# A relational graph kernel whose head is rearranged: which queue brings the constants, how early loads are sent, and in which slots seeds, message weight and looks stand

## The chip, the cores and the metric

The kernel runs on one core of one Trainium2 chip, in one launch. The metric is device time in microseconds (us). Before the change it is 169.39, the median of 3 runs (169.31 to 169.51). Engines are TensorE (PE), VectorE (DVE), ScalarE (ACT), GpSimd (POOL) and SyncE (SP). Five instruction streams run at once and meet only at semaphores.

## The reference

There are 128 graphs of 128 nodes with 128 features, and an adjacency matrix of integers for each. In this data its entries are 0 and 1. The reference computes two layers:

```
vals = (x @ W_loop.T + b_loop) * sigmoid((x @ W_loop.T) @ Wg_loop.T + bg_loop)
x1   = layernorm(x  + relu(adj_t(==1)  @ vals))          # other relations: entries 2..40
out  = layernorm(x1 + (adj(==1) @ x1) @ W_msg[0] + bias)   # other weights: entries 2..4
```

The layer norms are over features, without scale and shift. Entries above 1 are served by a general path (behind a flag) that this data doesn't take; the "looks" below are the check for it.

## The kernel before, in words

The 128 graphs are worked in 32 groups of 4, so a tile is 128 partitions x 512 float32 values (256 KB). Every engine walks the same loop of slots, t = 0 to 31. In slot t the stages stand for different groups, with lags written out by hand:

- `project(t)` (PE, L379): for each graph x_t times `w_gate` (128 x 256) into `hg_ps`, which has two halves used in turn. The left half of `w_gate` is `w_loop_t`; the right half is the product `w_loop` x `wg_t`, folded by PE at the start and copied by DVE (L641). The matmul accumulates onto biases that were written into `hg_ps` beforehand: the seed (ACT, L515, `seed`; for half of group 0 also DVE, L638), a copy of `gate_b`. A seed of group q may only be written when the `vals` of group q-2 have been taken from the same half.
- `gates(t)` (ACT, L524): sigmoid of the right part. `values(t)` (DVE, L727): the product `vals`.
- `loop_sum(t-1)` (PE, L391): adjacency times `vals`. `first_sum` (DVE, L735): relu and the addition of x, giving `s_sb`. `first_stats` (L742), the chain of small operations for the inverse root (L665 to L691, `chain`), and `norm1` (POOL, L320 and L328) give x1.
- `messages(t-3)` (PE, L409), `copy_messages` (ACT, L534), `message_weights(t-4)` (PE, L430), `second_sum` (DVE, L753), `second_stats` (L757), `norm2` (ACT, L551, in two halves `(0, 1)` and `(2, 3)`), and the store (SP, L258).
- `look(t)` (ACT, L560) squares the adjacency less one half and sums it, to find entries above 1.

PE's order in a slot is project, loop_sum, message_weights, messages. ACT's is copy_messages, half of norm2, gates(t), seed(t+1), the other half of norm2, look(t). In DVE's slots the whole inverse-root chain stands before `values` while there is no second sum (up to slot 4).

The weight of the second layer, `w1`, is centred by `message_weight` (DVE, L647 to L656, waiting on `w1_in`), one PE matmul with a constant matrix (L440, in slot 2) and `message_weight_end` (L661). DVE does the first in slot 1, between `values(1)` and `first_sum(0)`, and the last in slot 3.

Loads: SP sends `wg_t`, then x_t and x alternately into rings of 6 (L245, L250), one after another until the rings make it wait. ACT sends `w_loop`, `gate_b` (the biases) and `w_loop_t`, and after the first seed `w_msg`, `msg_bias` (`b1`) and `identity`. POOL waits for the two fold weights (`fold_in`, L334), then sends adjacency and transposed adjacency in pairs of groups (512 KB, L303, L310), the first five at once, and one more in each slot. PE begins with matmuls on a constant tile `warm`, 4 before `marked`, 3 more, and 3 after the fold.

Of the kernel before, what the change touches and what calls it, by code (L numbers as in the profile page):

```python
# [45 lines left out]
def exists(q):  # L46
    return 0 <= q < GROUPS
# [12 lines left out]
def build(nc, x, x_t, adj, adj_t, w_in, w_loop_t, wg_loop_t, gate_bias, w_msg, msg_bias,  # L60
          w_rel_t, wg_rel_t, b_rel, bg_rel, w_msgs, rel_ids, identity, out):
    with ExitStack() as ctx:
# [30 lines left out]
        w_gate = sb("w_gate", [P, 2 * P], F32)  # L93
        w_loop = sb("w_loop", [P, P], F32)
        wg_t = sb("wg_t", [P, P], F32)
        w1_raw = sb("w1_raw", [P, P], F32)
        w1 = sb("w1", [P, P], F32)
        b1 = sb("b1", [P, P], F32)
# [4 lines left out]
        warm = sb("warm", [P, W], BF16)  # L103
# [11 lines left out]
        ident = sb("ident", [P, P], F32)  # L115
# [27 lines left out]
        w_gate_in = sem("w_gate_in")  # L143
        fold_in = sem("fold_in")
        w1_in = sem("w1_in")
# [33 lines left out]
        ident_in = sem("ident_in")  # L179
# [61 lines left out]
        def _(sp):  # L241
# [21 lines left out]
            load_x(0)  # L263
            load_xt(2)
            load_x(1)
            load_xt(3)
# [30 lines left out]
        def _(pool):  # L297
# [35 lines left out]

            pool.wait_ge(fold_in, 16 * 2)  # L334
            load_adj(0)
            load_adj(1)
# [20 lines left out]
        def _(pe):  # L357
# [3 lines left out]
            for k in range(4):  # L361
                last = nc.tensor.matmul(bank[k], warm[:, 0:P], warm[:, :], start=True, stop=True)
# [4 lines left out]
            nc.tensor.matmul(aux_ps[:, 0:P], w_loop[:, :], wg_t[:, :], start=True, stop=True).then_inc(fold_done, 1)  # L367
# [6 lines left out]
            def project(q):  # L374
                if exists(q):
                    pe.wait_ge(xt_in[q % XT_RING], arrived(q, XT_RING))
                    pe.wait_ge(seeded, q + 1)
                    for b in range(GB):
                        last = nc.tensor.matmul(hg_ps[:, q % 2, b, :], xt_sb[:, q % XT_RING, batch(b)], w_gate[:, :],  # L379
                                                start=False, stop=True, skip_group_check=True)  # L380
                    last.then_inc(hg_done, 1)
# [31 lines left out]
            def message_weights(q):  # L413
                if exists(q):
                    if q == 0:
                        pe.wait_ge(w1_mid, 6)

                    if q in y_place:
                        pe.wait_ge(vals_done, GROUPS)
                    else:  # L420
                        await_count(pe, z_done, q)
                    if q >= LAST:
                        if q == LAST:
                            pe.wait_ge(ident_in, 16)
# [31 lines left out]
            def relation(step, ways):  # L456
                pe.wait_ge(rel_vals, step)
                for way in ways:
                    for b in range(GB):
                        last = nc.tensor.transpose(bank[way][:, batch(b)], gvals_t[:, way, batch(b)], ident[:, :])  # L460
# [39 lines left out]
        def _(act):  # L500
            act.dma_start(w_loop[:, :], w_in).then_inc(fold_in, 16)
            act.dma_start(gate_b[:, :], gate_bias).then_inc(bias_in, 16)
            act.dma_start(w_gate[:, 0:P], w_loop_t).then_inc(w_gate_in, 16)
# [51 lines left out]
            def look(q):  # L555
                spot = q // 2 % ADJ_RING
                act.wait_ge(adj_in[spot], arrived(q // 2, ADJ_RING))

                await_count(act, seen_done, q)
                nc.scalar.activation(seen[:, :], adj_sb[:, 2 * spot + q % 2, :], ACT.Square, bias=half[:, 0:1],  # L560
                                     accum_out=seen_sum[:, q:q + 1]).then_inc(seen_done, 1)

            seed(0)
            act.dma_start(w1_raw[:, :], w_msg).then_inc(w1_in, 16)
            act.dma_start(b1[:, :], msg_bias).then_inc(w1_in, 16)
            act.dma_start(ident[:, :], identity).then_inc(ident_in, 16)
            for t in range(GROUPS):
# [3 lines left out]
                seed(t + 1)  # L571
                norm2(t - NORM2_LAG, (2, 3))
                look(t)
# [53 lines left out]
        def _(dve):  # L627
# [13 lines left out]
            nc.vector.tensor_copy(w_gate[:, P:2 * P], aux_ps[:, 0:P]).then_inc(weights_ready, 1)  # L641

            def message_weight():


                dve.wait_ge(w1_in, 16 * 2)
                nc.vector.bn_stats(mid_stat[:, 0, :], w1_raw[:, :])  # L647
                nc.vector.bn_stats(mid_stat[:, 1, :], b1[:, :]).then_inc(w1_mid, 1)
# [156 lines left out]

            for t in range(GROUPS + 1):
# [82 lines left out]
            def general_pair(pair):  # L889
                dve.wait_ge(gadj_in, (pair + 1) * 32)  # L890
                for half_ in range(2):
# [25 lines left out]
                    for b in range(GB):  # L917
                        last = tt(gsum[:, batch(b)], gsum[:, batch(b)], b1[:, :], ALU.add)
# [56 lines left out]
```

## Time and profile before

| what | value |
|---|---|
| median of 3 runs | 169.39 us |
| profiled execution, its own time | 168.68 us |
| its span, first to last instruction | 166.9 us |
| busy share PE / DVE / ACT / POOL | 91% / 88% / 75% / 47% |
| mean granted TensorE clock | 0.985 of full speed |
| moved by DMA | 42.76 MB, mean 256 GB/s |
| share of the chain that ended last: PE / DMA / DVE | 78% / 8% / 7% |

The span is what the trace shows; the execution's time has 1.8 us around it. Shares of busy time are averages over a head, a long regular middle and a tail; which of them a change touches decides what it is worth. In the chain a piece is what the next one waited for. Start times are in us from the first instruction. A matmul of float32 data is recorded as two instructions, so four graphs give x8.

### The profile page before, as it was taken

The numbers are of one execution on the slowest core, as the hardware profiler recorded it, in microseconds if no ns is written. First come the engines' busy times: TensorE is split into PE (matmuls) and PEld (weight loads), VectorE is DVE, ScalarE is ACT, GpSimd is POOL, SyncE is SP. The second block draws the span as 40 slices with busy tenths as digits, with TensorE's granted clock in tenths as the row PEclk, the third lists the DMA queues.
The fourth block names the chain that finished last, engine by engine and source line by source line (L and its number), as shares of the span: only waits on it lengthen the run. The fifth ranks groups of instructions, "written<-read, shape, count | busy, mean of one in ns | idle before, by whom it ended". The sixth has DMA issues, their size and how long they took to land.

```text
span 166.9 us, 3913 instructions
## 1 busy us (share of the span) xinstructions
PE 151.6 (91%) x1072; PEld 140.4 (84%) x1072; DVE 146.7 (88%) x583; ACT 126.0 (75%) x287; POOL 78.6 (47%) x192
## 2 busy tenths in 40 slices
PE   6864899999999999999999999999999999998920
PEld 2553689999999999999999999999999999997910
DVE  1225999999999999999999999999999999999771
ACT  3266455679888888888888889998888888844661
POOL 2700366155555555565555555555554544446000
PEclk9999999999999999999999999999999999999985
DMA  4999999965999999999999899999995341131133
GB/s 137 342 389 394 397 401 403 308 196 189 298 302 306 310 304 274 280 312 301 268 305 329 272 277 333 325 310 298 253 324 212 85 166 63 65 130 63 64 125 138
DMA packets 19465, 42.76 MB, mean 256 GB/s; under 512 B 2160, under 2 KB 3056, under 8 KB 19440
## 3 DMA queue, kind: packets, MB, share of 16 engines
q1 hardware_dynamic: 13968, 25.24, 44.0%
q0 software_dynamic: 4608, 16.78, 33.2%
q10 hardware_dynamic: 864, 0.46, 0.9%
q8 instruction: 10, 0.16, 0.4%
q14 instruction: 15, 0.12, 0.3%
HBM read 34.08 MB, written 8.39 MB: 254 GB/s over the span
## 4 chain that ended last, share of the span: by engine, by line
PE 78%; DMA 8%; DVE 7%; issue 3%; ACT 1%; ACTq 0%; DVEq 0%
PE hg_ps L379 28%; PE msg_ps L409 16%; PE y_ps L430 15%; PE loop_ps L391 15%; DMA b<-msg_bias_dram 5%; DMA gate_b<-gate_bias_dram 2%; PE hg_ps L430 2%; PE hg_ps L426 2%; DVE s_sb L735 2%; DVE stats L742 1%; PE y_ps L426 1%; PE hg_ps L409 1%; ACT out_sb L551 1%; DVE z_sb L753 0%; DVE tiny L679 0%
## 5 line engine op out<-in xcount | busy, mean ns | idle before, releaser
L379 PE MATMUL hg_ps<-w_gate,xt_sb 128*128 128x256 f32 x256 | 60.8, 380 | 2.6 <-ACT hg_ps L515 2.5
L328 POOL TENSOR_SCALAR x<-s_sb,rstd,nmr 128x128 f32<-128x128 f32 x125 | 54.7, 446 | 3.7 <-DVE rstd L691 0.4
L379 PEld LDWEIGHTS hg_ps<-w_gate,xt_sb 128*128 128x128 f32 x256 | 46.2, 190 | 8.5 <-issue 3.0
L320 POOL TENSOR_TENSOR nmr<-mean_neg,rstd 128x4 f32<-128x4 f32 x31 | 6.0, 194 | 68.8 <-DVE rstd L691 68.8
L551 ACT ACTIVATE out_sb<-z_sb,rstd 128x128 f32<-128x128 f32 x112 | 38.0, 391 | 0.2 <-DVE rstd L691 0.2
L391 PEld LDWEIGHTS loop_ps<-vals,adj_sb 128*128 128x128 f32 x256 | 33.3, 191 | 5.2 <-issue 3.8
L391 PE MATMUL loop_ps<-vals,adj_sb 128*128 128x128 f32 x256 | 34.0, 276 | 2.6 <-DVE s_sb L735 2.6
L524 ACT ACTIVATE gate<-hg_ps 128x512 f32<-128x512 f32 x32 | 19.1, 597 | 22.2 <-PE hg_ps L379 22.1
L515 ACT ACTIVATE hg_ps<-gate_b 128x1024 f32<-128x1024 f32 (+1 forms) x32 | 32.3, 1010 | 1.0 <-DMA gate_b<-gate_bias_dram 1.0
L409 PE MATMUL msg_ps<-adjt_sb,x 128*128 128x128 f32 x248 | 33.0, 276 | 0.0
L430 PE MATMUL y_ps<-w,msg_t 128*128 128x128 f32 x232 | 30.6, 275 | 0.0
L409 PEld LDWEIGHTS msg_ps<-adjt_sb,x 128*128 128x128 f32 x248 | 30.2, 192 | 0.2 <-issue 0.2
L430 PEld LDWEIGHTS y_ps<-w,msg_t 128*128 128x128 f32 x232 | 28.2, 192 | 0.0
L727 DVE TENSOR_TENSOR vals<-hg_ps,gate 128x512 f32<-128x512 f32 x32 | 22.0, 688 | 6.4 <-ACT gate L524 5.7
L742 DVE BATCH_NORM_STATS2 stats<-s_sb 128x6 f32<-128x256 f32 x64 | 26.5, 426 | 0.3
L757 DVE BATCH_NORM_STATS2 stats<-z_sb 128x6 f32<-128x256 f32 x56 | 23.7, 427 | 0.0
L560 ACT ACTIVATE seen<-adj_sb,half 128x512 bf16<-128x512 f32 x32 | 22.7, 710 | 1.3 <-DMA adj_sb<-adj_dram 1.3
L534 ACT ACTIVATE msg_t<-msg_ps 128x512 f32<-128x512 f32 x31 | 18.0, 581 | 6.6 <-PE msg_ps L409 6.6
L735 DVE SCALAR_TENSOR_TENSOR s_sb<-loop_ps,x_sb 128x512 f32<-128x512 f32 x32 | 21.8, 682 | 0.0
L753 DVE TENSOR_TENSOR z_sb<-y_ps,x 128x512 f32<-128x512 f32 x28 | 19.1, 682 | 0.0
L303 POOL DMA_DIRECT2D adj_sb<-adj_dram x16 | 9.6, 598 | 2.8 <-DMA wg_t<-wg_loop_t_dram 2.8
L310 POOL DMA_DIRECT2D adjt_sb<-adj_t_dram x16 | 9.5, 591 | 0.0
(66 smaller groups left out, 104.9 us busy)
## 6 DMA issues: line engine op xcount, KB each, us to landing
xt_sb<-x_t_dram SPq DMA_DIRECT2D x32, 256.0 KB, 4.9
x_sb<-x_dram SPq DMA_DIRECT2D x32, 256.0 KB, 5.0
adj_sb<-adj_dram POOLq DMA_DIRECT2D x16, 512.0 KB, 5.5
adjt_sb<-adj_t_dram POOLq DMA_DIRECT2D x16, 512.0 KB, 5.2
out<-out_sb SPq DMA_DIRECT2D x32, 256.0 KB, 4.1
gate_b<-gate_bias_dram ACTq DMA_DIRECT2D x1, 128.0 KB, 3.4
w_loop<-w_loop_dram ACTq DMA_DIRECT2D x1, 64.0 KB, 2.0
wg_t<-wg_loop_t_dram SPq DMA_DIRECT2D x1, 64.0 KB, 2.2
```

Of the source, the lines that this page charges most:

```text
L328: last = nc.gpsimd.tensor_scalar(x1[:, q % X1_RING, batch(b)], s_sb[:, q % S_RING, batch(b)], r[:, b:b + 1], n[:, b:b + 1], ALU.mult, ALU.add)
L379: last = nc.tensor.matmul(hg_ps[:, q % 2, b, :], xt_sb[:, q % XT_RING, batch(b)], w_gate[:, :], start=False, stop=True, skip_group_check=True)
L391: last = nc.tensor.matmul(loop_ps[:, batch(b)], adj_sb[:, spot, batch(b)], vals[:, q % 2, batch(b)], start=True, stop=True)
L409: last = nc.tensor.matmul(msg_of(q)[:, batch(b)], x1[:, q % X1_RING, batch(b)], adjt_sb[:, spot, batch(b)], start=True, stop=True)
L430: last = nc.tensor.matmul(y_of(q)[:, batch(b)], msg_t[:, q % 2, batch(b)], w1[:, :], start=q < LAST, stop=True, skip_group_check=q >= LAST)
L515: nc.scalar.activation(hg_ps[:, q % 2, 0:graphs, :], gate_b[:, None, :].broadcast_to([P, graphs, 2 * P]), ACT.Copy).then_inc(seeded, 1)
L551: last = nc.scalar.activation(out_sb[:, q % OUT_RING, batch(b)], src, ACT.Copy, scale=r)
L560: nc.scalar.activation(seen[:, :], adj_sb[:, 2 * spot + q % 2, :], ACT.Square, bias=half[:, 0:1], accum_out=seen_sum[:, q:q + 1]).then_inc ...
L727: tt(vals[:, q % 2, :].rearrange("p (b n) -> p b n", b=GB), hg_ps[:, q % 2, :, 0:P], gate[:, q % 2, :].rearrange("p (b n) -> p b n", b=GB) ...
L735: stt(s_sb[:, q % S_RING, :], loop_ps[:, :], 0.0, x_sb[:, q % X_RING, :], ALU.max, ALU.add)\
L742: got = nc.vector.bn_stats(stats[:, (q + NORM1_LAG) % STATS_RING, p, :], s_sb[:, q % S_RING, 2 * p * P:2 * (p + 1) * P].rearrange("p (i n) ...
L757: got = nc.vector.bn_stats(stats[:, (q + STAT2_LAG) % STATS_RING, 2 + p, :], z_sb[:, q % Z_RING, 2 * p * P:2 * (p + 1) * P].rearrange("p ( ...
```

## The change

- Inputs are joined on the host: `w_loop` and `w_loop_t` to `w_loop_both` (one transfer of 128 KB into `w_all`, whose last third takes the folded product); `w_msg`, `msg_bias` and `identity` to `consts` (one transfer of 192 KB into `const_sb`).
- POOL no longer waits for the fold weights. It sends `gate_b`, `consts` and adjacency 0, waits for x_t 1, and then sends the other first loads. In the loop it sends both kinds of adjacency in odd slots, none in even ones.
- ACT sends only `w_loop_both`.
- SP waits for x_t 0 before it sends x_t 2, for x_t 1 before x 1, and for adjacency 0 before x_t 3 and all that follows.
- DVE does `message_weight` before slot 0 and `message_weight_end` at the end of slot 1. The matmul between them stands on PE in slot 1 before loop_sum(0).
- ACT seeds groups 0 and 1 before slot 0, and group t+2 at the end of slot t. `look(t - 1)` stands before that seed, and the last look after the loop.
- `warm` is a quarter as wide and is read repeatedly; of the matmuls on it 4 + 2 are left of 4 + 3 + 3.

```diff
 # SP
             load_xt(0)
             load_xt(1)
             load_x(0)
+
+            sp.wait_ge(xt_in[0], 16)
             load_xt(2)
+            sp.wait_ge(xt_in[1], 16)
             load_x(1)
+            sp.wait_ge(adj_in[0], 16)
             load_xt(3)
...
 # POOL
-            pool.wait_ge(fold_in, 16 * 2)
+            pool.dma_start(gate_b[:, :], gate_bias).then_inc(bias_in, 16)
+            pool.dma_start(const_sb[:, :], consts).then_inc(consts_in, 16)
             load_adj(0)
+            pool.wait_ge(xt_in[1], 16)
             load_adj(1)
...
-                if t % 2 == 0:
+                if t % 2 == 1:
                     load_adj(t // 2 + 3)
-                else:
                     load_adjt(t // 2 + 2)
...
 # PE
-            for _ in range(3):
-                nc.tensor.matmul(aux_ps[:, :], warm[:, 0:P], warm[:, :], start=True, stop=True)
             pe.wait_ge(fold_in, 16 * 2)
-            for _ in range(3):
-                nc.tensor.matmul(msg_ps[:, :], warm[:, 0:P], warm[:, :], start=True, stop=True)
-            pe.wait_ge(w_gate_in, 16)
+            for _ in range(2):
+                nc.tensor.matmul(msg_ps[:, :], warm[:, :], warm_wide, start=True, stop=True)
...
                 project(t)
+                if t == 1:
+                    pe.wait_ge(w1_mid, 3)
+                    nc.tensor.matmul(aux_ps[:, P:2 * P], share[:, :], w1_raw, start=True, stop=True)\
+                        .then_inc(w1_mean, 1)
                 loop_sum(t - LOOP_LAG)
-                if t == 2:
-                    pe.wait_ge(w1_mid, 3)
-                    nc.tensor.matmul(aux_ps[:, P:2 * P], share[:, :], w1_raw[:, :], start=True, stop=True)\
-                        .then_inc(w1_mean, 1)
...
 # ACT
-            act.dma_start(w_loop[:, :], w_in).then_inc(fold_in, 16)
-            act.dma_start(gate_b[:, :], gate_bias).then_inc(bias_in, 16)
-            act.dma_start(w_gate[:, 0:P], w_loop_t).then_inc(w_gate_in, 16)
+            act.dma_start(w_all[:, 0:2 * P], w_loop_both).then_inc(fold_in, 16)
...
             seed(0)
-            act.dma_start(w1_raw[:, :], w_msg).then_inc(w1_in, 16)
-            act.dma_start(b1[:, :], msg_bias).then_inc(w1_in, 16)
-            act.dma_start(ident[:, :], identity).then_inc(ident_in, 16)
+            seed(1)
             for t in range(GROUPS):
                 copy_messages(t - Y_LAG)
                 norm2(t - NORM2_LAG, (0, 1))
                 gates(t)
-                seed(t + 1)
                 norm2(t - NORM2_LAG, (2, 3))
-                look(t)
+                look(t - 1)
+                seed(t + 2)
+            look(GROUPS - 1)
...
 # DVE
+            message_weight()
             for t in range(GROUPS + 1):
...
-                if t == 1:
-                    message_weight()
-                if t == 3:
-                    message_weight_end()
...
                 step(CHAIN_OPS)
+                if t == 1:
+                    message_weight_end()
```

## Rows read from the trace of the kernel before

**Rows 1.** Busy time by stretches; columns: stretch, length, engines (instructions), granted clock, DMA share, GB/s.
```profile
1.00:5.00 4.00, 3.40 (x10) 1.65 (x11) 0.94 (x6) 1.69 (x3) 1.60 (x3) 1.00 0.73 220
5.00:24.00 19.00, 14.04 (x78) 11.28 (x76) 10.97 (x41) 10.05 (x18) 5.55 (x14) 1.00 1.09 384
...
30.00:60.00 30.00, 29.97 (x217) 28.39 (x217) 29.69 (x120) 25.23 (x56) 15.66 (x39) 1.00 0.84 271
```
**Rows 2.** The chain of waits, the middle; columns: start, us, what.
```profile
85.05 1.73 PE hg_ps L379 x8
...
89.45 1.73 PE hg_ps L379 x8
```
**Rows 3.** The chain of waits, the head up to 26 us.
```profile
1.31 3.40 DMA gate_b<-gate_bias_dram
...
5.17 9.18 DMA b<-msg_bias_dram
...
14.38 0.29 DVE mid_stat L647
...
15.91 0.69 DVE s_sb L735
...
24.58 1.13 PE loop_ps L391 x8
```
**Rows 4.** Instructions in order of time, 0 to 16 us; start, us, what [idle before].
```profile
0.88 0.39 SPq L260 DMA_DIRECT2D wg_t<-wg_loop_t_dram  x1
...
5.76 1.59 PEld L379 LDWEIGHTS hg_ps<-w_gate,xt_sb 128*128 128x128 f32 x8 [0.53 <-DMA w_gate<-w_loop_t_dram]
...
7.79 0.60 ACT L524 ACTIVATE gate<-hg_ps 128x512 f32<-128x512 f32 x1 [2.40 <-PE hg_ps L379]
...
8.29 1.02 ACT L515 ACTIVATE hg_ps<-gate_b 128x1024 f32<-128x1024 f32 x1
8.42 0.69 DVE L727 TENSOR_TENSOR vals<-hg_ps,gate 128x512 f32<-128x512 f32 x1 [2.73 <-ACT gate L524]
...
9.45 1.97 PE L379 MATMUL hg_ps<-w_gate,xt_sb 128*128 128x256 f32 x8 [1.70 <-ACT hg_ps L515]
...
12.09 0.69 DVE L727 TENSOR_TENSOR vals<-hg_ps,gate 128x512 f32<-128x512 f32 x1 [2.97 <-ACT gate L524]
```
**Rows 5.** Instructions in order of time, 15 to 32 us.
```profile
23.55 0.28 DVE L661 TENSOR_TENSOR w<-b_mid,aux_ps 128x128 f32<-128x128 f32 x1
23.75 0.68 DVE L735 SCALAR_TENSOR_TENSOR s_sb<-loop_ps,x_sb 128x512 f32<-128x512 f32 x1
```
**Rows 6.** DMA: loads issued 35.29, 3.39, 3.20, 6.18 (us to landing); POOL's queue 3.4:7.3 (packets).
```profile
adjt_sb<-adj_t_dram POOLq DMA_DIRECT2D x1, 512.0 KB, 3.5
...
adj_sb<-adj_dram POOLq DMA_DIRECT2D x1, 512.0 KB, 7.2
...
x_sb<-x_dram SPq DMA_DIRECT2D x1, 256.0 KB, 5.5
...
x_sb<-x_dram SPq DMA_DIRECT2D x1, 256.0 KB, 15.0
...
q0 software_dynamic: 1, 0.00, 0.5%
```
**Rows 7.** ACT's instructions in the middle, in order of time.
```profile
86.81 0.60 ACT L524 ACTIVATE gate<-hg_ps 128x512 f32<-128x512 f32 x1 [0.52 <-PE hg_ps L379]
```
**Rows 8.** Waits from 25 to 145 us: total, times, longest.
```profile
POOL nmr L320 <- DVE rstd L691: 51.4, 27, 3.5
```
**Rows 9.** Instructions in order of time, 141 us to the end.
```profile
145.18 0.71 ACT L560 ACTIVATE seen<-adj_sb,half 128x512 bf16<-128x512 f32 x1
...
146.78 0.60 ACT L534 ACTIVATE msg_t<-msg_ps 128x512 f32<-128x512 f32 x1 [0.80 <-PE msg_ps L409]
```
**Rows 10.** The warm-up matmuls of lines 362 and 369: ns min/median/max.
```profile
L362 PE MATMUL hg_ps<-warm x4: 606/634/634, 1.6 to 2.8; 128*128 128x512 bf16 x4
...
L369 PE MATMUL msg_ps<-warm x3: 379/379/379, 4.9 to 5.3; 128*128 128x512 bf16 x3
```

More of the change, by code:

```diff
@@ L57, in chain_end, with build @@
     return ((t - FIRST_CHAIN) // 2 + 1) * CHAIN_OPS
-def build(nc, x, x_t, adj, adj_t, w_in, w_loop_t, wg_loop_t, gate_bias, w_msg, msg_bias,
-          w_rel_t, wg_rel_t, b_rel, bg_rel, w_msgs, rel_ids, identity, out):
+def build(nc, x, x_t, adj, adj_t, w_loop_both, wg_loop_t, gate_bias, consts,
+          w_rel_t, wg_rel_t, b_rel, bg_rel, w_msgs, rel_ids, out):
     with ExitStack() as ctx:
@@ L91, in build @@
         last_rstd = sb("last_rstd", [P, 2, 2 * GB], F32)
-        w_gate = sb("w_gate", [P, 2 * P], F32)
-        w_loop = sb("w_loop", [P, P], F32)
+        w_all = sb("w_all", [P, 3 * P], F32)
         wg_t = sb("wg_t", [P, P], F32)
-        w1_raw = sb("w1_raw", [P, P], F32)
+        const_sb = sb("const_sb", [P, 3 * P], F32)
         w1 = sb("w1", [P, P], F32)
-        b1 = sb("b1", [P, P], F32)
         b1_mid = sb("b1_mid", [P, P], F32)
@@ L102, in build @@
         share = sb("share", [P, P], F32)
-        warm = sb("warm", [P, W], BF16)
+        warm = sb("warm", [P, P], BF16)
         half = sb("half", [P, 1], F32)
@@ L216, in y_of @@
             return y_place.get(q, y_ps[:, :])
+        w_loop, w_gate = w_all[:, 0:P], w_all[:, P:3 * P]
+        w1_raw, b1, ident = const_sb[:, 0:P], const_sb[:, P:2 * P], const_sb[:, 2 * P:3 * P]
+        warm_wide = warm[:, None, :].broadcast_to([P, GB, P])
         def batch(b):
@@ L361, in _ @@
             for k in range(4):
-                last = nc.tensor.matmul(bank[k], warm[:, 0:P], warm[:, :], start=True, stop=True)
+                last = nc.tensor.matmul(bank[k], warm[:, :], warm_wide, start=True, stop=True)
             last.then_inc(marked, 1)
-            for _ in range(3):
-                nc.tensor.matmul(aux_ps[:, :], warm[:, 0:P], warm[:, :], start=True, stop=True)
             pe.wait_ge(fold_in, 16 * 2)
-            nc.tensor.matmul(aux_ps[:, 0:P], w_loop[:, :], wg_t[:, :], start=True, stop=True).then_inc(fold_done, 1)
-            for _ in range(3):
-                nc.tensor.matmul(msg_ps[:, :], warm[:, 0:P], warm[:, :], start=True, stop=True)
-            pe.wait_ge(w_gate_in, 16)
+            nc.tensor.matmul(aux_ps[:, 0:P], w_loop, wg_t[:, :], start=True, stop=True).then_inc(fold_done, 1)
+            for _ in range(2):
+                nc.tensor.matmul(msg_ps[:, :], warm[:, :], warm_wide, start=True, stop=True)
             pe.wait_ge(weights_ready, 1)
@@ L378, in project @@
                     for b in range(GB):
-                        last = nc.tensor.matmul(hg_ps[:, q % 2, b, :], xt_sb[:, q % XT_RING, batch(b)], w_gate[:, :],
+                        last = nc.tensor.matmul(hg_ps[:, q % 2, b, :], xt_sb[:, q % XT_RING, batch(b)], w_gate,
                                                 start=False, stop=True, skip_group_check=True)
@@ L555, in look @@
             def look(q):
[L556 to L561, printed above, removed]
+                if exists(q):
+                    spot = q // 2 % ADJ_RING
+                    act.wait_ge(adj_in[spot], arrived(q // 2, ADJ_RING))
+                    await_count(act, seen_done, q)
+                    nc.scalar.activation(seen[:, :], adj_sb[:, 2 * spot + q % 2, :], ACT.Square, bias=half[:, 0:1],
+                                         accum_out=seen_sum[:, q:q + 1]).then_inc(seen_done, 1)
             seed(0)
-            act.dma_start(w1_raw[:, :], w_msg).then_inc(w1_in, 16)
-            act.dma_start(b1[:, :], msg_bias).then_inc(w1_in, 16)
-            act.dma_start(ident[:, :], identity).then_inc(ident_in, 16)
+            seed(1)
             for t in range(GROUPS):
@@ L917, in general_pair @@
                     for b in range(GB):
-                        last = tt(gsum[:, batch(b)], gsum[:, batch(b)], b1[:, :], ALU.add)
+                        last = tt(gsum[:, batch(b)], gsum[:, batch(b)], b1, ALU.add)
                     chain(last)
@@ L949 @@
         "adj_t": grouped(adj.transpose(0, 2, 1), 2 * GB),
[L950 to L951 removed]
+        "w_loop_both": _np.concatenate([w["L0_gnn_W_loop"], w["L0_gnn_W_loop"].T], axis=1),
         "wg_loop_t": _np.ascontiguousarray(w["L0_gnn_Wg_loop"].T),
         "gate_bias": _np.tile(gate_bias, (P, 1)),
[L954 to L955 removed]
+        "consts": _np.concatenate([w["L1_gnn_weight"][0], _np.tile(w["L1_gnn_bias"][None], (P, 1)),
+                                   _np.eye(P, dtype=_np.float32)], axis=1),
     }
```

30 lines of the change are left out of this document (11 added, 19 removed).

## The prediction, made before the changed kernel ran

> **What bounds the kernel now.** I read the busy time by stretches first. From 30 to 60 us TensorE (PE) is busy 29.97 of 30 us and VectorE (DVE) 29.69; from 5 to 24 us PE is busy only 14.04 of 19 and DVE 10.97 [rows 1]. So the middle is PE's and the loss is in the head. The chain of waits says what the middle costs: one projection follows the next at 85.05 and 89.45, 4.40 us a group, with nothing but matmuls between [rows 2]. What the head gains is therefore kept to the end, as long as the middle stays unbroken. The head's chain [rows 3] is: bias `gate_b` issued at 1.31, landed at 4.71; then `b1`, issued by ScalarE (ACT) at 5.17 and landed only at 14.35; then DVE's `message_weight`, 14.38 to 15.91; then the first `s_sb` at 15.91; and from the loop sum at 24.58 on PE never pauses. The figure to move is thus 24.58, and it hangs on the 15.91: the first `s_sb` sum starts at 15.91 and the third at 23.75 [rows 3, 5], 3.9 a slot, which is DVE's pace while PE isn't full.
>
> **The change part by part.** q counts groups; A is the start of projection 0, 5.76 now [rows 4].
>
> *Biases.* Now projection 0 starts 1.05 after `gate_b` lands (5.76 - 4.71): DVE's and ACT's seeds, then the copy of the folded weight. Both copies stay, and `w_loop` and `w_loop_t` become one transfer, so the wait on `w_gate` that ended last (0.53, rows 4) can go. `gate_b` moves from second on ACT's queue (1.31) to first on GpSimd's (POOL's). SP issues at 0.88 [rows 4]; I take 0.9 for POOL. No row shows a small transfer there. Bounds: a 512 KB one issued at 35.29 onto quiet queues landed in 3.5; the first, issued at 3.39 behind the six loads that SP had sent, took 7.2, and POOL's queue moved one packet between 3.4 and 7.3, some 4 us without data [rows 6]. So `gate_b` lands between 0.9 + 2.5 = 3.4 (estimate: less data than in the 3.5) and 0.9 + 4.0 + 1.0 = 5.9. Here it has ahead of it two small weights and one or two loads, nearest to the quiet row, and with more of it ahead but less data: I take its 3.5, landing at 4.4. A = 4.4 + 1.05 = 5.45, rounded to 5.5; ends 4.7 (the fold's own input and matmul) and 7.0.
>
> The Trainium skill ("DMA: Bandwidth & Descriptors", Latency and other measured facts) speaks against the move: a software-generated transfer from GpSimd starts some 0.4 us later than one from SP or ACT. The quiet row shows no more than such a difference, the loaded row ten times it; by that rule the sum below would be 0.4 us worse, 165.1.
>
> *Seeds two slots ahead.* Now ACT seeds q+1 after the gate of q: gate 0 at 7.79, seed 1 from 8.29 (1.02), and projection 1 waits 1.70 for it until 9.45; gate 1 waits for that projection and `vals` 1 starts at 12.09 [rows 4], A + 6.33. New: seeds 0 and 1 are there before, so projection 1 follows at once and ends at about A + 3.9. Gate 0 stays at A + 2.03, `vals` 0 runs A + 2.66 to A + 3.35; then seed 2 (it needs `vals` 0) to A + 4.4. Gate 1 stands behind it on ACT, later than projection 1's end: A + 4.4, and `vals` 1 from A + 5.05 to A + 5.7. The added wait costs 0.5 (3.9 to 4.4) of what the removed one gives. So the first `s_sb` can start at A + 5.7 = 11.2, if its loop sum is there.
>
> *Adjacency 0.* POOL now issues it third (about 2.1) instead of at 3.39, where it landed at 10.6 [rows 6]; the loop sum 0 must start by about 10.0. Quiet: 2.1 + 3.5 + some 1 for the two transfers ahead = 6.6; loaded: 2.1 + 7.2 = 9.3. Both are in time, so cost nothing; were it 10.6 again, the sum would lose 0.7. PE's one small share-matmul, now ahead of loop sum 0, has the 1.2 us between there and 11.2 as its cover.
>
> *Message weight early.* Its constants come as one 192 KB transfer, second on POOL, and its 1.53 us (14.38 to 15.91, rows 3) stand before `vals` 0. From 5.4 they end at 6.9; `vals` 0 starts at 5.5 + 2.66 = 8.15. Hidden behind projection 0, unless the constants land after 6.6; from there it costs one for one. Its end step (0.28 at 23.55, rows 5) moves from slot 3 to slot 1: nothing for the third `s_sb`. The 9.18 us of `b1` drop out of the chain. What is late next is `vals` 1.
>
> *From 11.2 on.* The first `s_sb` shifts by 15.91 - 11.2 = 4.7. Third `s_sb` and loop sum 3 follow by the same DVE work as before (23.75 - 15.91 = 7.84, then to 24.58), so PE is full from 19.9. PE's own work up to there (four projections of 1.9, three loop sums, messages 0) fits with small gaps.
>
> *Prefetch held back.* SP sends x_t 2 after x_t 0 has landed, x 1 after x_t 1, the rest after adjacency 0 (about 7). POOL sends its next loads after x_t 1. With both queues full, SP's loads landed at 8.7 (issued 3.20) and 21.2 (issued 6.18) with six steps between, 2.1 us each [rows 6]. New order from about 7.5: x 1 at 10, x_t 3 at 12.3, x 2 at 14.3, x_t 4 at 16.3, x 3 at 18.3. Needed, by the forecast: x_t 3 at 12.8, x_t 4 at 17.7, x 2 at 19.0, x 3 at 22.9. Nothing is late, by 0.5 at the closest; the cost is 0 to 2 (if POOL's packets go first) and I take 0.
>
> *Middle and tail.* ACT does the same work in another order and still has 0.52 us free before each gate [rows 7]. If the new order used it up, 25 groups would each lengthen (R5). POOL issues both adjacency loads in odd slots, one issue more there; it waits 51.4 us in 27 slots for DVE, 1.9 each [rows 8], so that is covered. The tail holds one more look (0.71 and the read of its sum) before the copy at 146.78, which has 0.80 idle before it [rows 9]: about 0.1, which I take as nothing; without the idle time it would be 0.9. The shorter memset gains nothing; 4 fewer warm-up matmuls are a rival.
>
> **Sum.** Gain 4.7. The profiled execution took 168.68, its span 166.9 and 1.8 around it; it becomes 164.0, span 162.2. The median of the runs is 0.7 above that execution: 169.39 - 4.7 = **164.7 us**.
>
> **The rivals.**
> - *R1, the bias is late on POOL.* For it: the 4 us without data [rows 6]. Against: that was behind six loads, here one or two. A = 7.0, first `s_sb` 12.7, gain 3.2: **166.2**.
> - *R2, PE at half rate in projections 0 and 1.* The granted clock reads 1.00, which is the 2.4 GHz level, in the head's stretches [rows 1]. Yet the first warm-up matmuls take 634 ns and the last three, of the same shape, 379 [rows 10], after PE had been busy from 1.6 us on. New: four fewer of them, and holes around the fold. Against: after the holes of 1.7 us now, projections still ran at the fast rate. Price: projection 0 alone at twice 1.73 delays everything by 1.7, gain 3.0; both, gain 1.3: **166.4 to 168.1**. The Trainium skill ("TensorE: Matmul & The Clock Gate", Part 1) has the array start at half clock and rise after sustained activity; durations agree, the granted-clock row doesn't.
> - *R3, SP's loads starve* because POOL's six 512 KB loads enter first: one step of 2.1 more puts x_t 3 at 14.4 (1.6 late, half of it covered, since loop sum 2 waits for DVE until 15.8) and x_t 4 at 18.4 (0.7 late), about 1.3 to 1.5 in all. For it: the steps of 2.1. Against: SP's queue, sent first, was the one served first in [rows 6]. **166.1**.
> - *R4, slower.* `message_weight` now stands ahead of `vals` 0 on DVE. Constants landing at C put `vals` 0 at C + 1.53, and by the steps above the first `s_sb` at C + 4.6. It decides from C = 11.3 (15.91 - 4.6): beyond that it is slower than before, at C = 12.5 by 1.2: **170.6**. For it: `b1` took 9.18, and 1.5 + 9.2 = 10.7 is close. Against: that was with all prefetch in flight, which is now held back.
> - *R5, no gain:* the middle gives it back, each of 25 groups 0.19 longer, once ACT's 0.52 is gone. **169.4.** Against: total ACT work is unchanged and the seed now has a slot to spare.
>
> **How the numbers follow.** Forecast 0.60 (163.6 to 165.6), R1 0.14, R2 0.11, R3 0.09, R4 0.03, R5 0.03. Faster (beyond 0.2%, about what a measurement of this kernel tells from no change) 0.94, same 0.03, slower 0.03. The range reaches over R1, R3 and the light half of R2: 163.5 to 167.2.
>
> **What would show it.** `gate_b` landing near 4.4; projection 0 near 5.5, projection 1 right behind with no wait on L515's seed; `message_weight` over before `vals` 0; first `s_sb` near 11.2; PE without pause from near 19.9, then 4.40 a group. Wrong if DVE waits for the constants, if PE waits for x_t or adjacency, if projections 0 or 1 take twice 380 ns a matmul, or if the period of the middle isn't 4.40.

## The result, and the profile after

The changed kernel takes 167.47 us (median of 4 runs, 166.99 to 167.7) against 169.45 (median of 4, 169.31 to 169.56) on the same chip: ratio 0.9879, 95% interval 0.9858 to 0.99. It is faster by 2.0 us; 4.7 were forecast, and 167.47 lies above the range. Every ratio in this document leaves out runs more than 1.5% above the fastest of the same kernel, among them one of e3 that took 323.07 us for no known reason; the medians of the table keep them. The profiled execution took 167.70 with a span of 166.0, the top of its runs, while that of before lay at the bottom of its own; so the two traces differ by 0.9 in span where the medians differ by 2.0.

The stretches come first; columns as in [rows 1].

```profile
1.00:5.00 4.00, 3.44 (x8) 1.11 (x8) 0.41 (x5) 1.49 (x2) 1.81 (x3) 1.00 0.59 163
5.00:24.00 19.00, 16.22 (x78) 13.66 (x78) 11.89 (x43) 10.13 (x17) 6.67 (x16) 1.00 1.03 354
...
30.00:60.00 30.00, 30.00 (x218) 28.51 (x217) 29.63 (x120) 25.39 (x56) 16.75 (x41) 1.00 0.91 304
```

From 5 to 24 us PE is busy 16.22 us with 78 matmuls; as many, nearly all of them the same, took it 14.04 before [rows 1]: 2.2 us more for almost the same work. The middle is full, as before. The chain of waits shows the new head and the unchanged period (88.43 - 84.02 = 4.41):

```profile
1.39 4.89 DMA gate_b<-gate_bias_dram
...
7.33 6.50 PE hg_ps L381 x16
...
19.80 1.13 PE loop_ps L393 x8
...
23.61 1.13 PE loop_ps L393 x8
...
84.02 1.73 PE hg_ps L381 x8
...
88.43 1.73 PE hg_ps L381 x8
```

`b1` is gone from it, and loop sum 3 stands at 23.61 where 24.58 stood [rows 3]. Two links of it are longer than forecast: the bias, and projections 0 and 1 (line 381). The head in order of time, columns as in [rows 4]:

```profile
1.39 0.72 POOL L338 DMA_DIRECT2D gate_b<-gate_bias_dram  x1 [0.81 <-POOLq L964]
...
6.39 0.69 DVE L638 COPY hg_ps<-gate_b 128x512 f32<-128x512 f32 x1 [4.98 <-DMA gate_b<-gate_bias_dram]
...
7.33 6.49 PE L381 MATMUL hg_ps<-w_all,xt_sb 128*128 128x256 f32 x16 [2.23 <-DVE w_all L641]
...
8.12 0.53 POOL L308 DMA_DIRECT2D adj_sb<-adj_dram  x1 [4.91 <-DMA xt_sb<-x_t_dram]
...
8.50 0.29 DVE L656 TENSOR_TENSOR b_mid<-b_mid,const_sb 128x128 f32<-128x128 f32 x1
...
13.85 0.60 ACT L524 ACTIVATE gate<-hg_ps 128x512 f32<-128x512 f32 x1 [0.32 <-PE hg_ps L381]
...
15.09 0.68 DVE L735 SCALAR_TENSOR_TENSOR s_sb<-loop_ps,x_sb 128x512 f32<-128x512 f32 x1
```

The reader is to see that DVE idles 4.98 us for the bias, that PE idles 2.23 behind it, that the message weight is over at 8.79 while projection 0 still runs, and that the 16 matmuls of two projections run without a hole, yet take 6.49 us. The matmuls of line 381 by piece (ns min/median/max) say why:

```profile
L381 PE MATMUL hg_ps<-w_all,xt_sb x3: 634/634/796, 7.3 to 8.3; 128*128 128x256 f32 x3
...
L381 PE MATMUL hg_ps<-w_all,xt_sb x3: 380/557/634, 12.2 to 13.0; 128*128 128x256 f32 x3
```

They run at half rate until about 12.6, then at 380 ns.

### The profile page after: what moved, and what is told of

Same layout as the page of the kernel before. It is cut to its first block, busy times and chain, and to the rows that moved or that the text cites. A ratio compares the mean times of both kernels' runs of the same rounds, so it can differ in the third digit from the quotient of the medians.

```text
span 166.0 us, 3902 instructions
## 1 busy us (share of the span) xinstructions
PE 153.1 (92%) x1068; PEld 141.9 (85%) x1068; DVE 145.5 (88%) x583; ACT 126.2 (76%) x287; POOL 79.9 (48%) x194
## 4 chain that ended last, share of the span: by engine, by line
PE 85%; DVE 5%; issue 3%; DMA 3%; ACT 1%; ACTq 0%; DVEq 0%; POOLq 0%
PE hg_ps L381 33%; PE msg_ps L411 16%; PE loop_ps L393 15%; PE y_ps L432 15%; DMA gate_b<-gate_bias_dram 3%; PE hg_ps L432 2%; PE hg_ps L428 2%; DVE s_sb L735 1%; ACT gate L524 1%; PE y_ps L428 1%; PE hg_ps L411 1%; ACT out_sb L551 1%; DVE stats L742 0%; DVE hg_ps L638 0%; DVE z_sb L753 0%
## 5 line engine op out<-in xcount | busy, mean ns | idle before, releaser
L381 PE MATMUL hg_ps<-w_all,xt_sb 128*128 128x256 f32 x256 | 63.3, 393 | 2.2 <-DVE w_all L641 2.2
L381 PEld LDWEIGHTS hg_ps<-w_all,xt_sb 128*128 128x128 f32 x256 | 48.2, 198 | 8.9 <-DVE w_all L641 3.1
L315 POOL DMA_DIRECT2D adjt_sb<-adj_t_dram x16 | 8.7, 545 | 0.0
```

## The experiments

In every kernel measured the rest of the span behind loop sum 3 is nearly the same: 166.9 - 24.58 = 142.3 before, 142.4 after, and between 141.9 and 142.8 in all the others below. So the start of loop sum 3 shows what the head did, but in one execution only: the same kernel, traced twice, had it at 23.61 and at 22.87. Differences of the three columns of starts are thus readings of single traces, good for the mechanism and rough as a size; only the ratio says what an edit is worth in time. The kernel before ran beside each group of runs, with medians of 168.55 (e1 to e4), 168.76 (e5 to e8) and 168.79 (e9, e10, after again), and each ratio is taken against those, so medians of different rows don't compare directly. All in us; "late x_t" is how long PE waits for an x_t load ahead of a projection (its number in brackets).

| kernel | median | ratio to before, 95% | projection 0 | first s_sb | loop sum 3 | late x_t |
|---|---|---|---|---|---|---|
| before | 169.39 | 1 | 5.76 | 15.91 | 24.58 | |
| after | 167.47 | 0.9879 (0.9858-0.9900) | 7.33 | 15.09 | 23.61 | |
| after again | 166.60 | 0.9853 (0.9812-0.9894) | 6.99 | 14.35 | 22.87 | 0.41 (3) |
| e1 bias on ACT | 165.80 | 0.9818 (0.9780-0.9856) | 5.62 | 13.19 | 21.71 | |
| e2 more warm-ups | 165.88 | 0.9843 (0.9792-0.9895) | 7.33 | 12.80 | 21.91 | 1.46 (3) |
| e3 both | 165.26 | 0.9791 (0.9747-0.9835) | 5.55 | 12.11 | 21.57 | 1.29 (1), 0.87 (4) |
| e4 nothing held | 166.69 | 0.9827 (0.9764-0.9889) | 6.46 | 13.55 | 22.10 | |
| e5 e3, nothing held | 166.27 | 0.9800 (0.9749-0.9850) | 5.66 | 11.51 | 21.83 | 0.58, 0.77, 1.05, 0.17 (1 to 4) |
| e6 e3, only POOL held | 165.07 | 0.9761 (0.9728-0.9794) | 5.61 | 11.61 | 20.14 | 0.74 (1) |
| e7 before + ACT's order | 168.98 | 1.0003 (0.9981-1.0024) | 6.26 | 15.53 | 24.45 | |
| e8 before + early consts | 167.34 | 0.9896 (0.9871-0.9922) | 6.72 | 15.14 | 23.81 | |
| e9 e6, consts on ACT | 165.84 | 0.9838 (0.9801-0.9874) | 5.86 | 13.15 | 21.68 | 0.14 (1) |
| e10 e6, message weight late | 166.39 | 0.9844 (0.9810-0.9878) | 5.86 | 14.61 | 23.27 | 2.02 (1) |

**The theories.** Mine after the result: the bias on POOL is late, PE waits for it with nothing to do, and that wait also leaves it at half rate; put the bias back on ACT and both go. The rival: the half rate has its own cause, the four warm-up matmuls taken away.

**e1, the bias back on ACT's queue, second.**

```diff
-            pool.dma_start(gate_b[:, :], gate_bias).then_inc(bias_in, 16)
...
             act.dma_start(w_all[:, 0:2 * P], w_loop_both).then_inc(fold_in, 16)
+            act.dma_start(gate_b[:, :], gate_bias).then_inc(bias_in, 16)
```

> The changed kernel with one edit: gate_b is sent by ACT, second behind w_loop_both, instead of first by POOL. Theory T (two causes: the bias comes late over POOL's queue, and PE, idle while it waits, works projections 0 and 1 at half rate): gate_b lands near 4.6 instead of 6.28, projection 0 starts near 5.7 instead of 7.33. If the half rate comes from the idle time before it (2.2 us in the changed kernel, then under 1), it goes too: first s_sb near 11.4 instead of 15.1, time near 164.5. Rival W (the half rate comes from the missing warm-up matmuls, not from the wait): projections 0 and 1 still take 6.5 together, first s_sb near 13.9, time near 166. Rival D (the held-back loads make everything late and the queue of gate_b matters little): time within 0.3 of the changed kernel.

In order of time:

```profile
4.68 0.70 DVE L638 COPY hg_ps<-gate_b 128x512 f32<-128x512 f32 x1 [3.28 <-DMA gate_b<-gate_bias_dram]
...
5.62 6.29 PE L380 MATMUL hg_ps<-w_all,xt_sb 128*128 128x256 f32 x16 [0.51 <-DVE w_all L641]
...
13.19 0.68 DVE L735 SCALAR_TENSOR_TENSOR s_sb<-loop_ps,x_sb 128x512 f32<-128x512 f32 x1
```

The bias lands at 4.6, projection 0 starts at 5.62 (5.5 forecast), and the first `s_sb` comes 1.90 earlier. But the 16 matmuls still take 6.29 us, with only 0.51 idle ahead of them. So the long wait for the bias was not what kept PE slow: my theory falls on that point. In time the step is small: 0.9818 (0.9780-0.9856) against 0.9879 (0.9858-0.9900), and the interval of the change measured again, 0.9812-0.9894, overlaps e1's.

**e2, ten warm-up matmuls behind the fold's instead of two,** the bias left on POOL.

```diff
-            for _ in range(2):
+            for _ in range(10):
                 nc.tensor.matmul(msg_ps[:, :], warm[:, :], warm_wide, start=True, stop=True)
```

> The changed kernel with one edit: 10 instead of 2 warm-up matmuls after the fold, so that PE is busy from 3.4 to about 7.3 while it waits for the bias. gate_b stays late. Theory T and rival W: projections 0 and 1 run at the fast rate (380 ns a matmul, 3.5 us for both instead of 6.5), first s_sb near 13.1 instead of 15.1, time 2 us less than the changed kernel, near 165.5. Rival D: the rate rises, but x_t, x or adjacency 0 (landed 9.3) is late next; gain under 0.7.

Line 381 and the same line in order of time:

```profile
L381 PE MATMUL hg_ps<-w_all,xt_sb x8: 379/379/379, 7.3 to 8.8; 128*128 128x256 f32 x8
```
```profile
7.33 3.62 PE L381 MATMUL hg_ps<-w_all,xt_sb 128*128 128x256 f32 x16
...
16.22 1.99 PE L381 MATMUL hg_ps<-w_all,xt_sb 128*128 128x256 f32 x8 [1.46 <-DMA xt_sb<-x_t_dram]
```

Projection 0 starts at 7.33 in both kernels, and the two projections take 3.62 instead of 6.49: the first `s_sb` comes 2.29 earlier for the warm-ups alone (1.55 against the second trace of the change, 14.35). By the ratios, 0.9843 (0.9792-0.9895) against 0.9879 and 0.9853, e2 isn't told apart from the change. (Here the bias landed at 5.4; the ten themselves ended only at 7.3, so they are too many.) A new wait shows: x_t 3 is 1.46 late.

**e3, both,** with warm-ups in three places: four, three ahead of the wait for the fold weights, three behind the fold.

```diff
+            for _ in range(3):
+                nc.tensor.matmul(aux_ps[:, :], warm[:, :], warm_wide, start=True, stop=True)
             pe.wait_ge(fold_in, 16 * 2)
...
-            for _ in range(2):
+            for _ in range(3):
```

> Both: gate_b on ACT's queue and the warm-up matmuls of the kernel before (4, 3, fold, 3). This is the case that the forecast described. Theory T: projection 0 near 5.8 at the fast rate, first s_sb near 11.5, PE full from near 20.2, time 164.5 to 165. Rival D: loads or the middle give back more than 1 us, time 166 or more.

In order of time:

```profile
8.84 1.99 PE L382 MATMUL hg_ps<-w_all,xt_sb 128*128 128x256 f32 x8 [1.29 <-DMA xt_sb<-x_t_dram]
...
12.11 0.68 DVE L737 SCALAR_TENSOR_TENSOR s_sb<-loop_ps,x_sb 128x512 f32<-128x512 f32 x1
...
19.73 1.99 PE L382 MATMUL hg_ps<-w_all,xt_sb 128*128 128x256 f32 x8 [0.87 <-DMA xt_sb<-x_t_dram]
```

And its chain of waits:

```profile
2.13 7.44 DMA adj_sb<-adj_dram
...
10.43 9.26 DMA xt_sb<-x_t_dram
```

Both gains are there, and what is late next takes a share: 15.09 - 1.90 - 2.29 + 1.29 = 12.19, against 12.11. That the sum fits to 0.1 is partly luck: from the second trace of the change it is 14.35 - 1.16 - 1.55 + 1.29 = 12.93. The 1.29 is x_t 1. Further on it is x_t 4: adjacency 0 lands at 9.57, SP may then go on, sends x_t 4 at 10.43, and that takes 9.26. So loop sum 3 stands at 21.57, only 0.14 ahead of e1's 21.71, where the first `s_sb` was ahead by 1.08 (13.19 - 12.11). From here on the late x_t loads bind, x_t 4 by way of the held prefetch. By its ratio e3 (0.9747-0.9835) is clear of the change's first interval (0.9858-0.9900), but not of its second (0.9812-0.9894).

**e4, the change without its four holding waits;** bias and warm-ups as in the change.

```diff
-            sp.wait_ge(xt_in[0], 16)
             load_xt(2)
-            sp.wait_ge(xt_in[1], 16)
             load_x(1)
-            sp.wait_ge(adj_in[0], 16)
...
             load_adj(0)
-            pool.wait_ge(xt_in[1], 16)
```

> The changed kernel without the three waits that hold the prefetch back (SP's on x_t 0, x_t 1 and adjacency 0, and POOL's on x_t 1). Theory T: the waits matter little by themselves; gate_b and the constants have the same queue ahead of them when they are sent, time within 0.5 of the changed kernel, unless SP's early loads delay gate_b as they delayed the first adjacency load of the kernel before (then gate_b near 7 and time up by 0.5 to 1). Rival D: the waits leave the DMA engines idle early on (153 GB/s from 4 to 5 us) and cost; without them the time falls by 1 us or more.

```profile
6.46 5.24 PE L377 MATMUL hg_ps<-w_all,xt_sb 128*128 128x256 f32 x16 [1.46 <-DVE w_all L637]
```

That row, in order of time, has the bias landing at 5.4 (issue to landing 4.0) and the half rate over sooner. Loop sum 3 at 22.10 is not later than the unaltered change's 23.61 and 22.87; part of that is the bias, whose landing differs from run to run by as much, so by itself this run does not price the waits. It does exclude that they are what gains.

**e5 and e6, e3 without waits.** e5 takes out all four, e6 only SP's three, so that POOL still waits for x_t 1.

> The kernel with gate_b on ACT and ten warm-up matmuls, and without the four waits that hold the prefetch back. In that kernel with the waits, x_t 1 was late by 1.3 us (projection 1 from 8.84) and x_t 4 by 0.9 (issued at 10.43, landed at 19.7), and loop sum 3 came at 21.7 instead of the 19.9 of the forecast. Theory H (the held-back loads cost these): x_t 3 and x_t 4 are sent at 3.7 and 5.6, PE waits for no x_t from slot 3 on, loop sum 3 near 20.3, time 1 us less than with the waits, near 164.2. Rival F (without the waits the bias, the constants or adjacency 0 come late again): adjacency 0 lands after 10.5 or the constants after 7, loop sum 3 stays near 21.5, time within 0.3.

> The same, but POOL keeps its wait for x_t 1 before adjacency 1; only SP's three waits are gone. Theory H: SP's loads for the first groups are all in flight before POOL's big ones enter, so x_t 3 and x_t 4 come earlier still; loop sum 3 near 20, time near 164 or the same as without any wait. Rival P (POOL's later loads, adjacency 1 and its transpose, become late: needed near 14.5 and 17): PE waits for adjacency in slot 3, time 0.5 or more above the kernel without any wait.

e5 in order of time:

```profile
12.11 1.99 PE L378 MATMUL hg_ps<-w_all,xt_sb 128*128 128x256 f32 x8 [0.77 <-DMA xt_sb<-x_t_dram]
...
16.05 1.99 PE L378 MATMUL hg_ps<-w_all,xt_sb 128*128 128x256 f32 x8 [1.05 <-DMA xt_sb<-x_t_dram]
```

e6 in order of time:

```profile
8.34 1.99 PE L379 MATMUL hg_ps<-w_all,xt_sb 128*128 128x256 f32 x8 [0.74 <-DMA xt_sb<-x_t_dram]
...
11.61 0.68 DVE L734 SCALAR_TENSOR_TENSOR s_sb<-loop_ps,x_sb 128x512 f32<-128x512 f32 x1
...
20.14 1.13 PE L391 MATMUL loop_ps<-vals,adj_sb 128*128 128x128 f32 x8
```

In e5 the first `s_sb` is the earliest of all, 11.51, but then every x_t load is late, and loop sum 3 is at 21.83, no better than e3. In e6 SP's loads queue up at once while all of POOL's 512 KB ones but the first come after x_t 1, and only x_t 1 is late: loop sum 3 at 20.14, where the prediction had 19.9, span 162.7 where it had 162.2. Its ratio lies 2.4% under before, and its interval is clear of both of the change's own. It has the lowest ratio found. In these traces, one execution each, POOL's wait is worth 1.7 us (21.83 - 20.14) and SP's three cost 1.4 (21.57 - 20.14). The times don't confirm these sizes: e3 and e5 at 0.9791 (0.9747-0.9835) and 0.9800 (0.9749-0.9850) overlap e6 at 0.9761 (0.9728-0.9794), so what the waits are worth in time isn't shown.

**e7, before with ACT's new order alone;** **e8, before with the constants' three loads first on POOL.**

```diff
+            seed(1)
             for t in range(GROUPS):
...
-                seed(t + 1)
...
-                look(t)
+                if t > 0:
+                    look(t - 1)
+                seed(t + 2)
+            look(GROUPS - 1)
```
```diff
 # POOL, ahead of its first wait
+            pool.dma_start(w1_raw[:, :], w_msg).then_inc(w1_in, 16)
+            pool.dma_start(b1[:, :], msg_bias).then_inc(w1_in, 16)
+            pool.dma_start(ident[:, :], identity).then_inc(ident_in, 16)
...
 # ACT, behind seed(0)
-            act.dma_start(w1_raw[:, :], w_msg).then_inc(w1_in, 16)
...
```

> The kernel before with ACT's order alone changed: seeds 0 and 1 ahead of slot 0, seed t+2 and look t-1 at the end of slot t. Theory T: the first s_sb is held by message_weight, which waits for b1 until 14.35, so the earlier projection 1 gains nothing there: s_sb at 15.9, time within 0.3 of the kernel before. b1 is sent after two seeds here, up to 1 us later, so s_sb may come up to 1 us later. Rival G (the seeds were a bound of their own): time 1 us or more lower. It also tells whether the new order costs in the middle: the period must stay 4.40.

> The kernel before with one edit: the three loads w_msg, msg_bias and identity are the first that POOL sends, instead of ACT's after seed 0. message_weight stays in slot 1, ACT's order is the old one. Theory T: b1 lands near 7, message_weight is over before vals 1 is, the first s_sb starts when vals 1 ends, at 12.8 to 14.4 (the 1.5 us of message_weight then stand behind vals 1): 1.5 to 3.1 us less, time 166.3 to 167.9 against 169.4. Rival G: something else (adjacency 0, x 0, the seeds) holds the first s_sb and less than 1 us comes.

e7 in order of time, then three pieces of it (busy time by stretches, and line 379):

```profile
14.00 0.29 DVE L650 BATCH_NORM_STATS2 mid_stat<-w_raw 128x6 f32<-128x128 f32 x1 [2.09 <-DMA b<-msg_bias_dram]
...
16.36 1.74 PE L391 MATMUL loop_ps<-vals,adj_sb 128*128 128x128 f32 x8 [3.19 <-DVE s_sb L738]
```
```profile
16.00:18.00 2.00, 1.64 (x9) 1.67 (x10) 1.83 (x9) 0.00 (x0) 0.00 (x0) 0.67 1.10 395
18.00:20.00 2.00, 2.00 (x7) 1.67 (x7) 1.86 (x7) 0.53 (x1) 0.97 (x3) 0.50 1.11 398
```
```profile
L379 PE MATMUL hg_ps<-w_gate,xt_sb x4: 634/634/634, 18.3 to 19.6; 128*128 128x256 f32 x4
```

The seeds alone gain nothing (1.0003), because `b1` still binds: DVE waits 2.09 us for it. PE then idles 3.19 us before loop sum 1 (1.66 in the kernel before), and behind that the granted clock is 0.67 and 0.50 (the 1.2 GHz level) with 634 ns a matmul. e8, DVE in order of time, and its bias load:

```profile
13.62 0.29 DVE L647 BATCH_NORM_STATS2 mid_stat<-w_raw 128x6 f32<-128x128 f32 x1
...
15.14 0.68 DVE L735 SCALAR_TENSOR_TENSOR s_sb<-loop_ps,x_sb 128x512 f32<-128x512 f32 x1
```
```profile
gate_b<-gate_bias_dram ACTq DMA_DIRECT2D x1, 128.0 KB, 4.3
```

And its projection 0:

```profile
6.72 1.97 PE L382 MATMUL hg_ps<-w_gate,xt_sb 128*128 128x256 f32 x8 [0.83 <-DMA w_gate<-w_loop_t_dram]
```

The constants no longer bind; the message weight starts in its place in slot 1. It gains 0.77 at loop sum 3 and 1% in the ratio, though `gate_b`, on ACT as before, now takes 4.3 instead of 3.4, and projection 0 starts at 6.72 for 5.76, behind `w_gate`, which is late too. Whether POOL's three early loads are the reason isn't shown: in e1, e3, e5, e6 and e10 POOL's queue had 192 and 512 KB under way, and `gate_b` on ACT took 3.2 to 3.3. What a reader should take from e8 is its ratio, 0.9896 (0.9871-0.9922): this one edit of the old kernel gets nearly what the whole change gets (0.9879 and 0.9853).

**e9, e6 with the constants third on ACT** and adjacency 0 first on POOL; **e10, e6 with the message weight back in slots 1 to 3.**

```diff
 # e9
-            pool.dma_start(const_sb[:, :], consts).then_inc(consts_in, 16)
...
+            act.dma_start(const_sb[:, :], consts).then_inc(consts_in, 16)
```
```diff
 # e10, DVE
-            message_weight()
             for t in range(GROUPS + 1):
...
+                if t == 1:
+                    message_weight()
+                if t == 3:
+                    message_weight_end()
```

> The best kernel so far (gate_b on ACT, ten warm-ups, only POOL holds back its loads after adjacency 0) with consts too on ACT's queue, third behind gate_b; POOL's first load is adjacency 0. In the best kernel the constants land at 7.1 (5.7 after their issue on POOL), message_weight ends at 8.7 and vals 0 starts 0.45 after its gate is done. Theory T (POOL's first small transfers are slow to start): constants land near 5.5, vals 0 starts at 8.3, first s_sb up to 0.4 earlier (11.2), time 0.3 to 0.4 less, unless x_t 1, late already (projection 1 at 8.34), holds it: then within 0.2. Rival Q (adjacency 0's packets, four times as large as the constants', now enter first and push x_t 0 or x_t 1 back): projection 1 at 8.8 or later, time 0.3 or more above.

> The best kernel so far with message_weight back in slot 1 on DVE (between vals 1 and the first s_sb), its matmul in slot 2 and its end in slot 3, as in the kernel before; the constants still come early, so nothing is waited for. Theory T (early message_weight is hidden beside projection 0, late it stands on the path): vals 0 0.4 earlier, then 1.53 behind vals 1: first s_sb near 12.7 to 13.1 instead of 11.6, time 1.0 to 1.5 more. Rival R (its place doesn't matter once the constants are there, since PE or the loads bind): within 0.3.

e9, in order of time, and the matmuls of line 378 from 5.8 to 8:

```profile
5.86 4.69 PE L378 MATMUL hg_ps<-w_all,xt_sb 128*128 128x256 f32 x16
...
8.45 0.60 ACT L523 ACTIVATE gate<-hg_ps 128x512 f32<-128x512 f32 x1 [2.12 <-PE hg_ps L378]
...
8.72 0.29 DVE L646 BATCH_NORM_STATS2 mid_stat<-const_sb 128x6 f32<-128x128 f32 x1 [3.04 <-DMA const_sb<-consts_dram]
```
```profile
L378 PE MATMUL hg_ps<-w_all,xt_sb x7: 379/380/667, 5.9 to 7.8; 128*128 128x256 f32 x7
```

e10, in order of time:

```profile
9.82 1.99 PE L379 MATMUL hg_ps<-w_all,xt_sb 128*128 128x256 f32 x8 [2.02 <-DMA xt_sb<-x_t_dram]
...
13.09 0.28 DVE L646 BATCH_NORM_STATS2 mid_stat<-const_sb 128x6 f32<-128x128 f32 x1
...
14.61 0.68 DVE L734 SCALAR_TENSOR_TENSOR s_sb<-loop_ps,x_sb 128x512 f32<-128x512 f32 x1
```

In e9 the constants take 6.9 us from issue, `message_weight` starts at 8.72, and `vals` 0 waits for it until 10.25: loop sum 3 is 1.54 later than in e6. Of the 1.59 by which `vals` 0 is later (8.66 in e6) the constants account for 1.2, since gate 0 ended at 9.05. The rest is something else: in e9 the first matmuls of projection 0 ran at half rate, although all ten warm-ups were there. The 1.2 is R4's mechanism, at a size far below its price. (The expectation calls adjacency 0's packets four times as large as the constants'; in the trace they have 4096 bytes against 1536, and projection 1 at 8.56 stayed below rival Q's 8.8.) In e10 the first `s_sb` is 3.00 later than in e6: 1.52 are the message weight between 13.09 and 14.61, and 1.48 the load of x_t 1, which landed later in this execution (9.82 - 8.34) and has nothing to do with the edit. So making the weight early is worth the 1.5 us of its own length; the ratios, 0.9844 against 0.9761 with intervals that don't overlap, put e10 0.8% or 1.4 us behind e6.

**The change again, unaltered,** beside e9 and e10.

> The changed kernel once more, unaltered, beside the two above, to see how its time and its bias landing vary. Theory T: 166.9 to 167.8, gate_b's landing between 5.4 and 6.3 (it was 6.28 in its first trace and 5.4 in two kernels with the same first sends), projections 0 and 1 at half rate again (one matmul 634 ns). Rival: the half rate was chance of that one trace, and comes back at 380 ns.

In order of time, and its bias load:

```profile
6.99 5.72 PE L381 MATMUL hg_ps<-w_all,xt_sb 128*128 128x256 f32 x16 [1.98 <-DVE w_all L641]
```
```profile
gate_b<-gate_bias_dram POOLq DMA_DIRECT2D x1, 128.0 KB, 4.6
```

Both findings are there again, a little smaller: bias 4.6 instead of 4.9, the two projections 5.72 instead of 6.49, loop sum 3 at 22.87. The change's own gain thus varies between executions by some 0.7 us.

**Warm-ups and rate over all thirteen traces.** With six warm-up matmuls (after, after again, e1, e4) the first matmul at the full rate starts between 9.6 and 13.0 us, always inside the two projections. With ten (fourteen in e2) it starts between 4.1 and 7.2: before projection 0 in six, at its first or second matmul in e7 and e10, at its fourth in e9. The two groups don't overlap, so the warm-ups decide whether the projections run slow. With six, PE also idles 0.3 to 0.4 us ahead of the fold and 0.5 to 2.2 behind the last warm-up. e2 kept the first pause and filled the second; whether it is the number of warm-ups or work without the second pause that counts, no run separates.

## Why the prediction was wrong

The direction, the place and the length of the unaffected rest were right; the size was not. Two steps failed at once, and together they are the whole gap in the profiled execution: the first `s_sb` was forecast at 11.2 and came at 15.09, 3.9 later. In the second trace of the change it came at 14.35, later by 1.5 for the bias and 1.7 for the half rate. The medians miss by less, 2.8 us (167.47 against 164.7), because the trace of before lay low among its runs and that of after high.

- **Biases: the term was mis-sized (1.8 us).** The prediction had POOL issue at 0.9 and the load take the quiet row's 3.5. POOL issued at 1.39, and it took 4.89. Four executions with the bias first on POOL show 4.9, 4.6, 4.0 and 4.0; those of the changed kernel with it on ACT (e1, e3, e5, e6, e9, e10) 3.2 to 3.4. Landing was 6.28 instead of 4.4, projection 0 at 7.33 instead of 5.5; the 1.05 between them held. My error was to take a row from 35 us as near to a load sent at 1 us among others. The upper bound that I had worked out, A = 7.0, was the better figure, and even it was passed. The Trainium skill ("DMA: Bandwidth & Descriptors", Latency and other measured facts) has a transfer from GpSimd start some 0.4 us later; here the landing is 1.7 us later than ACT's 4.6, of which the issue is 0.1 (1.39 against 1.31) and the rest the transfer; over the four executions the transfer alone is 0.6 to 1.7 us longer.
- **"Seeds two slots ahead": its duration of projections 0 and 1 failed (2.1 us).** I let projection 1 end at A + 3.9; at half rate it ended at A + 6.5, and the first `s_sb` came at A + 7.76 instead of A + 5.7. I had this as R2 but judged it by what followed a hole in the old trace, where PE had ten warm-ups behind it, not six. e2, and e3 against e1, show the warm-ups to be the cause; e1 shows that the 2.23 us hole ahead of projection 0 isn't. How long the half rate lasts varies from execution to execution, and e9 had a little of it with ten.
- **R1 and R2 taken as alternatives.** Each had its chance, and a range that ended at one of them. Both came: 4.7 - 1.8 - 2.1 = 0.8, the 0.9 of the spans. Nothing in the profile excluded the one by the other.
- **"Prefetch held back, cost 0": right in the change, and only because the two others hid it.** With them removed, the holds cost 1.4 in the traces (e3 against e6); their ratios overlap. The prediction had adjacency 0, which opens SP's last wait, "about 7"; it landed at 9.3 in the changed kernel, which is what the prediction had worked out for a loaded queue, and at 9.57 in e3. R3 expected SP to starve; in e6, with POOL held, it doesn't but for x_t 1, and in e5, without, it does, by 0.17 to 1.05 each slot up to 4.
- **Seeds and the order on ACT: right.** Projection 1 follows with no wait for its seed, and 6.00 us lie between projection 0 and the first `s_sb` in e6 (5.61 to 11.61), the forecast's 5.7 and part of the 0.74 that x_t 1 is late. The stretch from there to loop sum 3 was right too: 8.5 to 8.7 in before, after, e1 and e6. What the earlier seeds give by themselves, with the constants in time, no run isolates.
- **Message weight: right.** It was over at 8.79, before `vals` 0 at 11.78, so it cost nothing; in e6 it ended at 8.74 and held `vals` 0 up by 0.4 (gate 0 ended at 8.24), which x_t 1, late anyway, covered. e10 gives its price in the old place, 1.5. The constants landed by 7.2, so R4's point of 11.3 was far off, but e9 shows that 8.7 already costs when the rest is quick.
- **Middle and tail: right.** The period is 4.41, and ACT's slack before the gate, 0.52 before [rows 7], reads so after:

```profile
85.79 0.60 ACT L524 ACTIVATE gate<-hg_ps 128x512 f32<-128x512 f32 x1 [0.51 <-PE hg_ps L381]
```

  In the tail the copy that had 0.80 idle before it [rows 9] now follows the look without a pause, and the rest behind loop sum 3 is as long as before (142.4 against 142.3). R5 is out.

The first `s_sb` at 11.2 and loop sum 3 at 19.9 were thus not wrong as a picture of what the new order can give: e6 comes to 11.61 and 20.14 with two changes of queue and warm-up and three waits fewer. They were wrong as a forecast of this change.

**What stays open.** Why x_t 1, issued at the same time, lands between 6.4 (after again) and 9.8 (e10) in these executions, and at 5.5 before (so that projection 1 never waited for it), isn't settled; it goes with POOL's loads sent early, but no run took just these away. Nor is it settled whether fewer than the ten warm-ups of e3 would do, or what makes the moment at which the rate rises vary. What the holding waits are worth in time is open too.

## What to carry to other kernels

Price the first transfers of a kernel from rows of its first microseconds, and put the one that everything waits for on a queue whose rows there are short. Trace a kernel twice before taking a difference under 1 us between two traces for the worth of an edit. Warm-up matmuls are no filler: before removing some, ask what rate the first real matmuls would have, and read it from their durations. And when two risks stand before the same result, work out the case in which both come; a wait that costs nothing while something else is late becomes the bound once that is mended.

## What the runs showed of the hardware

- The granted-clock column reads 1.00 (the 2.4 GHz level) for 1 to 5 and 5 to 24 us of the changed kernel, while its matmuls took 634 ns until 12.6 and 379 to 380 from 13.0 on. The reason lies in the trace: its first clock record, at full speed, stands at 12.96 us (at 4.83 before, 3.98 in e6, 7.16 in e9), and the column reads 1.00 wherever there is no record. So at the start of this program the half rate has to be read from durations. A later drop has its record: 0.67 and 0.50 in e7 at 16 to 20 us, after 3.19 us idle. The Trainium skill ("TensorE: Matmul & The Clock Gate", Part 1) says that the clock events of a profile are not always reliable, and that how many matmuls run slow at a kernel's start changes from run to run; the 6.49 and 5.72 us of two executions of the same kernel agree with the second, while no record here contradicts the durations.
- A load of 128 KB issued at 1.3 us took 3.2 to 3.4 us on ACT's queue in eight traces, and 4.3 in a ninth (e8, where POOL had three small loads first); issued at 1.4 on POOL's queue it took 4.0 to 4.9 in four. Among the first loads of this program the queue made a difference, and so did something that changes between executions.
